# A graph network on one core: carried sums fetched three blocks ahead, and mask and target of a carry block copied to PSUM before its three VectorE operations

## The reference, cut to what matters

```python
# layer 0 (batch is all zeros, so u_per_node is one row)
all_feat = concat([x[dst], x[src], edge_attr, u_per_node[dst]], -1)
msg = relu(all_feat @ W1 + b1)
agg = segment_sum(msg, dst, N)
x = layernorm(x + relu(concat([x, agg, u_per_node], -1) @ W2 + b2))
# layer 1: two convolutions, each followed by a batch norm
h = x @ W + b
agg = segment_sum(h[src] + (edge_attr @ We + be), dst, N) + h
h = batchnorm(relu(agg) + bias)
# output
layernorm(x + h)
```

## Time and profile before

| | us |
|---|---|
| median of 3 runs | 7802.66 (7797.47 to 7810.06) |
| the profiled execution | 7799.23 |
| its span, first to last instruction | 7797.5 |
| tables | to about 196 |
| edge part: cycle 0 | 196.3 to 445.3 |
| cycles 1 to 4 | 445.3 to 890.0 |
| cycles 5 to 37 | 890.0 to 4491.7 |
| cycle 38 and the last step | 4491.7 to 4600.8 |
| last carry blocks, node part | 4600.8 to about 5145 |
| two convolutions, output | about 5145 to 7797.5 |

### The profile page before, as it was taken

How to read it: one execution, slowest core, us unless ns; L and a number is a source line. 1 busy time by engine, 2 the same in 40 slices (tenths; PEclk the granted TensorE clock), 3 DMA queues, 4 the chain that set the end, 5 groups by cost and what they waited for, 6 DMA issues and landing times.

```text
span 7797.5 us, 166429 instructions
## 1 busy us (share of the span) xinstructions
PE 6012.8 (77%) x60257; PEld 5159.6 (66%) x60257; DVE 4425.6 (57%) x5943; ACT 2114.4 (27%) x5348; POOL 3965.5 (51%) x3933
## 2 busy tenths in 40 slices
PE   3177777777777777777777756689999999999996
PEld 3055555555555555555555546679999999999996
DVE  4168888888888888888888848840011111011113
ACT  1044444444444444444444400000000000000001
POOL 7777777777777777777777764410011110001111
PEclk7576666666666666666666666689999999999998
DMA  5157777777777777777777774569999998999996
GB/s 141 49 175 241 249 237 249 246 253 243 241 257 239 249 241 243 257 245 248 240 248 245 253 221 160 162 257 381 362 382 382 383 381 345 381 363 381 384 380 245
DMA packets 973999, 2113.94 MB, mean 271 GB/s; under 512 B 668085, under 2 KB 759691, under 8 KB 860003
## 3 DMA queue, kind: packets, MB, share of 16 engines
q1 hardware_dynamic: 809823, 1841.27, 63.4%
q0 software_dynamic: 136064, 258.22, 13.6%
q10 hardware_dynamic: 28030, 13.36, 0.9%
HBM read 1457.70 MB, written 654.73 MB: 271 GB/s over the span
## 4 chain that ended last, share of the span: by engine, by line
PE 48%; DVE 20%; issue 12%; DMA 10%; POOL 7%; DVEq 1%; SPq 1%; ACTq 0%; ACT 0%; POOLq 0%
PE psum L998 25%; PE psum L877 10%; DVE edge_area L1411 9%; POOL arena L703 5%; PE psum L852 4%; DMA arena<-adj 4%; PE psum L835 4%; PE psum L836 2%; DVE arena L1402 2%; DMA arena<-b_tab,arena 2%; DMA arena<-in_src_steps 2%; DVE edge_area L1416 1%; DVE arena L1419 1%; DVE arena L1416 1%; POOL arena L717 1%
## 5 line engine op out<-in xcount | busy, mean ns | idle before, releaser
L703 POOL DMA_INDIRECT arena<-b_tab,arena x3125 | 3116.1, 997 | 952.6 <-issue 936.4
L1411 DVE TENSOR_TENSOR edge_area<-psum,arena 128x1024 bf16<-128x1024 f32 x2368 | 2487.4, 1092 | 625.0 <-PE psum L852 624.9
L1127 ACT CAST arena<-psum 128x392 bf16<-128x392 f32 x4736 | 1921.0, 505 | 2113.8 <-PE psum L852 2088.0
L998 PE MATMUL psum<-arena 128*128 128x192 bf16 x29008 | 2446.0, 246 | 29.2 <-DMA arena<-adj 20.9
L998 PEld LDWEIGHTS psum<-arena 128*128 128x128 bf16 x29008 | 2400.5, 98 | 38.0 <-issue 35.2
L852 PE MATMUL psum<-edge_area 64*128 64x98 bf16 x18944 | 1226.1, 241 | 464.8 <-ACT arena L1127 456.9
L765 POOL DMA_INDIRECT arena<-a_carry,a_carried x196 | 185.4, 946 | 2397.3 <-DVE arena L1629 1386.6
L835 PE MATMUL psum<-w_edge,arena 96*128 96x288 f32 x1250 | 677.3, 638 | 885.2 <-DVE arena L1402 885.2
L852 PEld LDWEIGHTS psum<-edge_area 64*128 64x128 bf16 x18944 | 782.3, 110 | 711.3 <-issue 683.1
L1595 DVE TENSOR_REDUCE arena<-psum 128x64 f32<-128x192 f32 x296 | 104.2, 352 | 1698.0 <-PE psum L998 1112.6
L835 PEld LDWEIGHTS psum<-w_edge,arena 96*128 96x128 f32 x1250 | 268.7, 268 | 962.3 <-issue 962.3
(11 more groups left out here) (248 smaller groups left out, 3185.3 us busy)
## 6 DMA issues: line engine op xcount, KB each, us to landing
arena<-adj SPq DMA_DIRECT2D x592, 1568.0 KB, 8.8
adj<-arena SPq DMA_DIRECT2D x296, 1568.0 KB
q_tab<-arena SPq DMA_DIRECT2D x312, 480.0 KB
edge_area<-q_tab SPq DMA_DIRECT2D x117, 768.0 KB
arena<-in_edge_t_steps SPq DMA_DIRECT2D x312, 192.0 KB
over_area<-q_tab SPq DMA_DIRECT2D x78, 768.0 KB
arena<-b_tab,arena POOLq DMA_INDIRECT x3125
over_area<-m_cont SPq DMA_DIRECT2D x196, 48.0 KB
```

Of the source, the lines that this page charges most:

```text
L703: nc.gpsimd.indirect_dma_start(rows[:, us, k, S - 1 - s, :], None, b_tab[:, :], bass.IndirectOffsetOnAxis(ap=index[:, us, 1 - k, s:s + 1], ...
L998: one = mm(psum[:, h, 0:3 * F], ring[:, r, n, :], xs[l][:, k, :], start=(k == 0 and not own), stop=(k == NB - 1))
L1127: copy(stage[:, h2, h, :, column:column + BATCH], psum[:, 2 + 2 * b + h, 0:BATCH * NB].rearrange("p (e n) -> p n e", n=NB)).then_inc(kept, 1)
L1411: one = V.tensor_tensor(to[:, d, :, :], over(lanes, [P, HOT, n], 1), over(code, [P, HOT, n], 2), ALU.is_equal)
```

## The change

Three things. First, GpSimd issues the first three carried sums of the node part ahead, and then the one for block b+3 where that for block b stood. Second, in `over_terms` (the 196 carry blocks alone; `node_term` is as it was) VectorE waits until its own operations on the block before are finished, copies the mask (16 values, bf16 to fp32) and the target row (64 values) of the block to a free stretch of PSUM bank 6, and waits for the copies. Third, `window_terms` gets these two PSUM operands in place of the SBUF ones.

```diff
+AHEAD = 3
...
+        over_mask_ps = psum[:, 6, 256:256 + WM]
+        over_add_ps = psum[:, 6, 256 + WM:256 + WM + F]
...
             pool.wait_ge(m_carry_out, 16 * MOB)
+            for b in range(AHEAD):
+                gather_carry(b)
             for b in range(NB):
-                gather_carry(b)
+                if b + AHEAD < NB:
+                    gather_carry(b + AHEAD)
                 if b + WIN < NB:
                     gather_window(b + WIN)
...
                 dve.wait_ge(a_w_in[n], c * 16 + 16)
-                window_terms(order_of_over(b), over_win[n % 2 if buffer is None else buffer], m_mask[:, some(b, 1), :].rearrange("p o i -> p (o i)"), a_w[:, n, :])
+                wait(dve, relued, order_of_over(b))
+                wait(dve, masked, order_of_over(b))
+                V.tensor_copy(over_mask_ps, m_mask[:, some(b, 1), :].rearrange("p o i -> p (o i)")).then_inc(over_terms_laid, 1)
+                V.tensor_copy(over_add_ps, a_w[:, n, :]).then_inc(over_terms_laid, 1)
+                dve.wait_ge(over_terms_laid, b * 2 + 2)
+                window_terms(order_of_over(b), over_win[n % 2 if buffer is None else buffer], over_mask_ps, over_add_ps)
```

More of the change, by code:

```diff
@@ L279, in build @@
         over_target_made = sem("over_target_made")
+        over_terms_laid = sem("over_terms_laid")
         halved = sem("halved")
```

## The result

| | before | after |
|---|---|---|
| median, us | 7800.82 (5 runs, 7797.42 to 7810.06) | 7766.07 (5 runs, 7762.08 to 7771.04) |
| ratio | | 0.9955, 95% interval 0.9941 to 0.9970 |
| profiled execution | 7799.23 | 7763.87 |
| first VectorE add of the edge part | 196.3 | 197.3 |
| cycle 0 | 249.0 | 249.4 |

The changed kernel is 34.7 us faster, against 33 forecast. In the two profiled executions the difference is 35.4 us: 8.7 in cycles 1 to 4, 11.1 in cycle 38, 16.9 in the node part, and 1.4 lost before cycle 1. The five runs of each kernel lie 9 to 13 us apart, so a single us of these means little. The lines have moved: L703 is L708, L1402 is L1410, L1411 is L1419, L1416 to L1419 are L1424 to L1427, the copies are L1451 and L1452, L852 is L860, L936 is L944, L1532 is L1545.

A forecast was written before the change was run, and what follows sets the result against it. The TensorE, ScalarE, VectorE loop, in step with TensorE's clock rises, was taken to bound the edge part's middle, GpSimd cycle 38, VectorE the node part; 7 + 10 + 16 = 33 us less gives 7769 us, range 7748 to 7808.

The forecast's parts named there:

- Copies, 0.34 us a block: Carry blocks: two copies to PSUM and the wait for them take 0.34 us of VectorE, bounds 0.2 and 0.5.
- Absorbed in cycles 5 to 37: Edge part, cycles 5 to 37: earlier clock rises after the add give the copies' time back; cost 0, otherwise 61 us.
- rival A: Stretch after each carry block, cycles 2 to 37: copies are paid in full, 61 us on top, 7831 us; chance 0.14.
- the beat: Edge-part loop: TensorE's clock rises 20.48 us apart, once a cycle 27.31, together the 109.23 us cycle; late work regains half.
- PSUM operands cost nothing: Carry blocks: the three VectorE operations keep their time with one operand in PSUM, 624 ns against 628; cost 0.
- GpSimd is freed: Gathers beside carry blocks are no longer stretched: GpSimd gets 3.0 us a middle cycle, about 4.1 in cycles 1 to 4.
- rival D: Carry blocks: PSUM operands do not free GpSimd; only the 16 us of the node part stay, 7787 us; chance 0.04.
- It does not shorten the middle: Middle cycles of the edge part: freeing GpSimd gains nothing, as VectorE does not wait for it; 109.2 us a cycle stay.
- rival B: Edge part, cycles 5 to 37: GpSimd sets the cycle, so freeing it saves 96 us more, 7674 us; chance 0.05.
- Cycles 1 to 4, 7 us: Start of the edge part: without gathers falling behind, the loop finds its beat earlier; 7 us less, between 0 and 7.8.
- Cycle 38, 10 us: Last edge cycle, whose end GpSimd sets: its 5.3 us count and it arrives ahead; 10 us less, between 5 and 13.
- Carried sums ahead, 15 and 1 us: Node part: twelve groups' shorter waits save 15 us, group 0 net 1 after the later sixth window; together 16, between 10 and 24.

The follow-up runs named there:

- the run with less work: The changed kernel with the mask multiplication in carry blocks covering one window slot of 16 instead of all; 7764.83 us, ratio 0.9952.
- the late sums: The changed kernel with a node group's sums taken one block later on VectorE, behind the next group's first term; 7731.07 us, ratio 0.9907.

## Why the prediction was right, point by point

**Copies, 0.34 us a block: right.** 0.32 measured, from start to start. The bound of 0.2 would have been too low, 0.5 too high; the slope of 1.0 ns a value held for such small operations.

**Absorbed in cycles 5 to 37: right, and so rival A falls.** 0.32 us x 5 x 33 = 53 us of work cost 0. The delay shrank by 0.66 to 0.73, about twice 0.32, as said. The three experiments on this one term agree from both sides: 0.48 us less a block gains nothing, 0.33 more costs 1.70 a cycle for 1.65 of work, 0.86 more costs 5.8 for 4.3. So the price is nothing up to an edge, and beyond it more than the work itself. Rival A's point was where the prediction put it, a little lower: with 5.10 us as the shortest delay seen, it had a cost of 0.5 us a block as the limit. Measured, 4.84 still meets its rise; the add behind it ends at 2877.09, 4.78 ahead of where the beat's next rise would be (2861.39 + 20.48), and misses it. So the edge is at about 4.8, which by (6.11 - 4.8) / 2 is a cost of 0.65 us a block. The change uses up over half of that room: the shortest delay of a cycle goes from 6.11 to 5.41. The prediction held that nothing in the trace had tried the absorption; cycles 1 to 4 had, as shown below.

**PSUM operands cost nothing: right.** L1424 takes 1.22 us as L1416 did. The Trainium skill, page "VectorE: DVE Perf Modes", section "Why PSUM operands drop a tier", has any fp32 operation with a PSUM operand at the single rate. The trace agrees: 1.22 us for 1024 elements with the operand in PSUM as in SBUF.

**GpSimd is freed: right, rival D falls.** Over 0.943 us a gather the stretch goes from 3.13 to 0.03 us a cycle with the operands in PSUM, and stays at 3.16 with the copies alone. The Trainium skill, page "SBUF — State Buffer", section "Who interferes with whom", says that a VectorE instruction with at most one SBUF input, outside its two-port modes, does not contend with GpSimd; by that rule all gathers beside the carry blocks should be plain, and in the edge part after cycle 0 none takes over 0.96 us.

**It does not shorten the middle: right, rival B falls.** 96 us came off GpSimd and none off the cycles. But the reason given, that GpSimd is full and still not late, hides how close it was: the second execution with the sums ahead alone lost 21 us there. So the PSUM operands also take away a risk, which no term of the sum has. (That was a single execution on another chip, where the kernel before has the widest range, 7796.1 to 7819.0; its trace shows the cause in the rises.) Of the kernel before, 41 timed runs in the three sets lie between 7793.5 and 7819.0, of the one with PSUM operands alone 11 lie between 7780.4 and 7785.8; that the wide spread comes from late rises, 3.41 us each, fits, but no trace was taken of the runs at its ends.

**Cycles 1 to 4, 7 us: the size right (8.7), the cause not.** The prediction counted the 4.1 us a cycle that GpSimd gets. The copies alone, with gathers still stretched, give 7.8 of the 8.7 (436.8 twice), and no run has unstretched gathers without the copies, so what the freed gathers would do by themselves is not shown. What the traces do show is late rises again. In the kernel before, the add of one step in cycle 3 waits 1.64 us for its gather and ends at 746.04; from there to the rise:

```profile
746.04:753.88 7.84, 7.70 (x54) 6.22 (x55) 4.92 (x6) 2.32 (x6) 5.92 (x7) 0.50 0.88 270
```

The rise of the beat, 3.41 us sooner, would have come 4.43 behind the add, and that is beyond the edge. Before has three such rises in cycles 1 and 3 (444.7 us), the carried sums alone three (445.6) and in the second execution two (442.7); the changed kernel, the PSUM operands alone, the copies alone and the run with less work have none (435.1 to 436.8). So the step that failed is the reasoning that the loop finds its beat earlier because GpSimd gets 4.1 us a cycle: what counts is that no add waits for a gather past the edge, and a later start of the three operations does that as well. That the size came out is in part luck.

**Cycle 38, 10 us: the size right** (11.1), within the ends of 5 and 13. But 3.6 to 3.9 of it come with the copies alone, which the prediction credited with nothing here; only the rest, some 7, is shown to need the PSUM operands.

**Carried sums ahead, 15 and 1 us: right.** 16.9 in all. Eleven of the twelve groups save about 1.2 each as said, and the third meets TensorE's product at a higher clock, 1.7 us instead of 3.4, and saves 3.1; the prediction had this as its bound of 24, in four groups. Group 0 saves 9.8 - 3.9, and the window's wait grows by 4.2 instead of 5.0; from the last add to the first sum of a group it is 55.9 us before and after, so the net there is 0 and not 1. The last group, which had no carried sum to wait for, shows the same 3.39 us as before: this row was what told how much of the 65.2 us was to be had. The experiment with the late sums shows it from the other side: the wait of 3.4 was TensorE behind VectorE's last term, and goes when a term stands in front of it.

**The sum was right by its terms**, with errors of 1.7, 1.1 and 0.9 us that go the same way, and 1.4 us more before cycle 1 against them. That it came within 2 us is better than the working deserves: the start of the edge part alone differs by up to 9 us between profiled executions, and the reason given for two of the terms held in part only.

## What to carry to other kernels

When an engine waits for the later of two, read what the second one would cost before counting the wait as won: a place where the first is absent by chance (here the last group) shows it. Where a loop has a period that a clock's rises make, work on its path costs nothing up to an edge and more than its own time beyond it, so measure the distance to the edge with an extra operation before adding or removing anything. And do not credit a gain to the freed engine alone when the edit also shifts the instructions: here the copies alone, with the gathers beside them still stretched, gave nearly the same 8 us in cycles 1 to 4.

## What the runs showed of the hardware that was not expected

- Two operands in SBUF against gathers on GpSimd: the stall depends on where the gather begins. Begun 0.04 to 1.07 us behind the start of a VectorE operation of about 1.22 us, it is done 2.03 to 2.05 us behind that start: 2.00 us long at worst, in place of 0.945.
- A gather that comes late costs more than its own delay where the loop keeps a beat: the add waited 1.23 us, and the rise came 3.41 us later than the beat's.
- Beyond the edge an added VectorE operation costs more than it lasts: 5.8 us a cycle for 4.3 of work, since TensorE stays at 1.2 GHz for 7.7 to 8.2 us behind the add instead of 5.4 to 6.1.
- The start of the edge part differs by 6 and 9 us between two executions of one kernel, each on another chip (204.0 and 198.1; 204.9 and 196.3).
